# Edge positions of the attention-score one-hots: one line in one partition, spread by a TensorE product

## The reference

```
def _gatv2_layer(x, src, dst, Wl, bl, Wr, br, att, b):
    n = x.shape[0]
    xl = (x @ Wl + bl).reshape(n, H, C)
    xr = (x @ Wr + br).reshape(n, H, C)
    s = jax.nn.leaky_relu(xl[src] + xr[dst], NEG_SLOPE)
    e = jnp.einsum('ehc,hc->eh', s, att)
    ...
```

## Time and profile before

| | us |
|---|---|
| median of 3 runs (3100.20 to 3102.39) | 3101.64 |
| the profiled execution | 3132.41 |
| its span in the trace | 3130.6 |
| the score stage's DVE instructions, layer 0 | from 655.8 |
| the same, layer 1 | from 1775.4 |

### The profile page before, as it was taken

One profiled execution on the slowest core, in us unless ns is written; L12 is line 12 of the kernel. 1 busy time (PEld: TensorE's weight loads), 2 busy tenths in 40 slices (PEclk: granted clock), 3 DMA queues, 4 the chain that ended last, 5 costly groups with the idle time before them and its releaser, 6 DMA issues. The chain is left out here.

```text
span 3130.6 us, 52451 instructions
## 1 busy us (share of the span) xinstructions
PE 2350.9 (75%) x12514; PEld 1551.1 (50%) x12628; DVE 2237.7 (71%) x10715; ACT 1249.0 (40%) x2770; POOL 826.8 (26%) x883
## 2 busy tenths in 40 slices
PE   3775796578888788737885788887788378857999
PEld 1443684234444444416664344444444156645777
DVE  5667666868888888884558688888888944466654
ACT  1776893332222222213354523222222123356654
POOL 0000100036666566500000265666665100000000
PEclk8999898789999999969997899999999689978999
DMA  0000600269999999617543489999988065436221
GB/s 26 1 2 3 282 7 15 91 202 277 276 278 275 271 274 278 193 29 177 159 111 83 159 266 273 277 275 282 275 274 270 4 155 160 137 86 251 80 64 38
DMA packets 418141, 519.14 MB, mean 166 GB/s; under 512 B 31943, under 2 KB 353090, under 8 KB 416450
## 3 DMA queue, kind: packets, MB, share of 16 engines
q0 software_dynamic: 66560, 274.39, 28.0%
q1 hardware_dynamic: 349996, 239.60, 26.4%
q10 hardware_dynamic: 1302, 1.80, 0.2%
HBM read 414.74 MB, written 100.93 MB: 165 GB/s over the span
## 5 line engine op out<-in xcount | busy, mean ns | idle before, releaser
L963 POOL DMA_INDIRECT rows<-row_table,idx x832 | 789.2, 949 | 813.5 <-POOLq L140 307.8
L1014 PE MATMUL z_ps<-xr,hot_ta 128*128 x2400 | 673.6, 388 | 246.1 <-DVE rows L1065 196.6
L1025 PE MATMUL z_ps<-rows,ident 128*128 128x256 f32 x1664 | 576.5, 428 | 10.4 <-issue 10.4
L1014 PEld LDWEIGHTS z_ps<-xr,hot_ta 128*128 128x128 bf16 x2496 | 245.0, 98 | 538.9 <-issue 407.9
L1065 DVE SCALAR_TENSOR_TENSOR rows<-rows,att_all 128x128 f32<-128x128 f32 x1664 | 429.5, 294 | 77.7 <-remote 37.1
L1090 DVE TENSOR_TENSOR rows<-z_ps,rows 128x256 f32<-128x256 f32 x832 | 347.5, 418 | 132.7 <-PE z_ps L1025 89.4
L1065 DVE SCALAR_TENSOR_TENSOR rows<-z_ps,att_all 128x128 f32<-128x128 f32 x1664 | 410.0, 280 | 25.5 <-issue 25.3
L1405 PE MATMUL acc_m<-xr,hot_m 128*128 x1984 | 341.2, 293 | 76.3 <-issue 53.2
L1405 PEld LDWEIGHTS acc_m<-xr,hot_m 128*128 128x128 f32 x1984 | 281.9, 194 | 142.0 <-issue 136.6
L1036 ACT ACTIVATE spread_a<-spread_a,below 128x512 bf16<-128x512 bf16 x208 | 149.9, 721 | 447.8 <-PE z_ps L1025 379.9
L1025 PEld LDWEIGHTS z_ps<-rows,ident 128*128 128x128 f32 x1664 | 257.3, 195 | 112.0 <-issue 18.3
(11 more groups left out here) (460 smaller groups left out, 3673.6 us busy)
## 6 DMA issues: line engine op xcount, KB each, us to landing
xr<-kept_rows SPq DMA_DIRECT2D x124, 512.0 KB
kept_rows<-rows SPq DMA_DIRECT2D x416, 128.0 KB
spread_a<-rel_rows SPq DMA_DIRECT2D x208, 128.0 KB
counts_line<-counts SPq DMA_DIRECT2D x1, 19550.0 KB
counts<-counts_line SPq DMA_DIRECT2D x6, 3200.0 KB, 10.0
rows<-row_table,idx POOLq DMA_INDIRECT x832
row_table<-xl_ring SPq DMA_DIRECT2D x50, 258.0 KB
rows<-row_table SPq DMA_DIRECT2D x32, 320.0 KB, 7.0
```

The lines of the kernel that those rows point to most:

```text
L963: nc.gpsimd.indirect_dma_start(out=rows[:, u, :], out_offset=None, in_=table, in_offset=bass.IndirectOffsetOnAxis(ap=c.idx[:, n:n + 1], ax ...
L1014: nc.tensor.matmul(ps[:, n % Z, :], hot, tile[:, m, 0:HC], start=m == 0, stop=False, skip_group_check=True)
L1025: nc.tensor.matmul(ps[:, n % Z, HALF_C:HC], c.ident[:, :], rows[:, n % ROWS, HALF_C:HC], start=False, stop=True, skip_group_check=True).th ...
```

## The change

SP loads the 512 numbers of a half as one line into one partition (`line`, four buffers, L971). PE multiplies a row of 128 ones (`one_row`, set once by DVE) with that line: a matmul with one row of weights and 512 columns, whose result, in the new PSUM bank `spread_ps`, holds the line in each of the 128 partitions. ACT's Abs reads that bank and writes the same `spread` buffer as before; Relu is unchanged. PE makes the products of halves 0 and 1 ahead of slot 0, and that of half k+2 in slot 4k+1, behind L1019 and ahead of the wait for the gather. It waits there for the Abs of the half before (`apart`), since there is one bank, and for the load (`line`). ACT waits for the product (`spread`, now one counter). SP's wait before a load is for the product that read the buffer. For the bank, `Z` goes from 6 to 5, so PE waits for slot n-5 instead of n-6.

```
--- before.py
+++ after.py
@@ -928,25 +928,29 @@
 
 
 
-    Z = 6
+    Z = 5
     ROWS = 14
     HOTS = 3
+    LINES = 4
     LOAD = HALF
     GROUPS = SLOTS // GROUP
     HALVES = SLOTS // HALF
     with ExitStack() as ctx:
         hot_t = ctx.enter_context(nc.sbuf_tensor(fresh(nc, "hot_ta"), [P, HOTS, HALF * P], BF16))
         spread = ctx.enter_context(nc.sbuf_tensor(fresh(nc, "spread_a"), [P, HOTS, HALF * P], BF16))
+        line = ctx.enter_context(nc.sbuf_tensor(fresh(nc, "rel_line"), [1, LINES, HALF * P], BF16))
+        one_row = ctx.enter_context(nc.sbuf_tensor(fresh(nc, "one_row"), [1, P], BF16))
         below = ctx.enter_context(nc.sbuf_tensor(fresh(nc, "below"), [P, 1], F32))
         part = ctx.enter_context(nc.sbuf_tensor(fresh(nc, "edge_part"), [P, 2, GROUP, H], F32))
         side = ctx.enter_context(nc.sbuf_tensor(fresh(nc, "side"), [P, 2, GROUP, PARTS, H], F32))
         half_sum = ctx.enter_context(nc.sbuf_tensor(fresh(nc, "half_sum"), [P, GROUP, H], F32))
         lin = ctx.enter_context(nc.sbuf_tensor(fresh(nc, "lin"), [P, 2, GROUP, H], F32))
         ps = ctx.enter_context(nc.psum_tensor(fresh(nc, "z_ps"), [P, Z, BANK], F32))
+        spread_ps = ctx.enter_context(nc.psum_tensor(fresh(nc, "spread_ps"), [P, BANK], F32))
         side_ps = ctx.enter_context(nc.psum_tensor(fresh(nc, "side_ps"), [P, 2, BANK], F32))
         rows = ctx.enter_context(nc.sbuf_tensor(fresh(nc, "rows"), [P, ROWS, ROW], F32))
 
-        with phase(nc, used=0, gathered=ROWS, spread=HOTS, below=0, apart=0, hot_t=0, z=0, sides=0, side=0, lin=0, added=0, summed=0,
+        with phase(nc, used=0, gathered=ROWS, line=LINES, one_row=0, spread=0, below=0, apart=0, hot_t=0, z=0, sides=0, side=0, lin=0, added=0, summed=0,
                    vec=0, kept=ROWS // 2) as (block, s):
 
 
@@ -968,18 +972,18 @@
             @block.sync
             def _(sp):
                 def load(k):
-                    sp.dma_start(spread[:, k % HOTS, :], bass.AP(rel_rows.tensor, k * HALF * P,
-                                                                 [[0, P], [1, HALF * P]]))\
-                      .then_inc(s["spread"][k % HOTS], 16)
-
-                for k in range(HOTS):
+                    sp.dma_start(line[:, k % LINES, :], bass.AP(rel_rows.tensor, k * HALF * P,
+                                                                [[HALF * P, 1], [1, HALF * P]]))\
+                      .then_inc(s["line"][k % LINES], 16)
+
+                for k in range(LINES):
                     load(k)
                 for n in range(0, SLOTS, 2):
                     k = n // HALF
-                    if n % HALF == 0 and k + HOTS < HALVES:
-
-                        sp.wait_ge(s["hot_t"], k + 1)
-                        load(k + HOTS)
+                    if n % HALF == 0 and k + LINES < HALVES:
+
+                        sp.wait_ge(s["spread"], k + 1)
+                        load(k + LINES)
                     at = n % ROWS
                     for u in range(at, at + 2):
                         sp.wait_ge(s["gathered"][u], 16 * (n // ROWS + 1))
@@ -996,6 +1000,17 @@
                         max_val=NODE_TILES - 1,
                         skip_runtime_bounds_check_because="slots hold node tiles by construction")[1]
 
+                def spread_rows_of(k):
+
+                    if k > 0:
+                        pe.wait_ge(s["apart"], k)
+                    pe.wait_ge(s["line"][k % LINES], 16 * (k // LINES + 1))
+                    nc.tensor.matmul(spread_ps[:, :], one_row[:, :], line[:, k % LINES, :], start=True, stop=True)\
+                      .then_inc(s["spread"], 1)
+
+                pe.wait_ge(s["one_row"], 1)
+                for k in range(HOTS - 1):
+                    spread_rows_of(k)
                 tiles_next = tiles_at(0)
                 for n in range(SLOTS):
                     u, k = n % GROUP, n // HALF
@@ -1021,6 +1036,8 @@
                         .rearrange("p (n k) -> p n k", n=PARTS), hot, tile[:, :, HC:XRW], start=True, stop=True)
                     if u == GROUP - 1:
                         last.then_inc(s["sides"], 1)
+                    if n % HALF == 1 and k + HOTS - 1 < HALVES:
+                        spread_rows_of(k + HOTS - 1)
                     pe.wait_ge(s["gathered"][n % ROWS], 16 * (n // ROWS + 1))
                     nc.tensor.matmul(ps[:, n % Z, HALF_C:HC], c.ident[:, :], rows[:, n % ROWS, HALF_C:HC],
                                      start=False, stop=True, skip_group_check=True).then_inc(s["z"], 1)
@@ -1029,11 +1046,11 @@
             def _(act):
                 def one_hot(k):
 
-                    act.wait_ge(s["spread"][k % HOTS], 16 * (k // HOTS + 1))
+                    act.wait_ge(s["spread"], k + 1)
                     if k >= HOTS:
                         act.wait_ge(s["z"], (k - HOTS + 1) * HALF)
                     mine = spread[:, k % HOTS, :]
-                    nc.scalar.activation(mine, mine, ACT.Abs, bias=below[:, 0:1]).then_inc(s["apart"], 1)
+                    nc.scalar.activation(mine, spread_ps[:, :], ACT.Abs, bias=below[:, 0:1]).then_inc(s["apart"], 1)
                     act.wait_ge(s["apart"], k + 1)
                     nc.scalar.activation(hot_t[:, k % HOTS, :], mine, ACT.Relu, bias=1.0, scale=-1.0)\
                       .then_inc(s["hot_t"], 1)
@@ -1082,6 +1099,7 @@
                             out=c.e[:, k * GROUP:(k + 1) * GROUP, 0:H], in0=part[:, k % 2, :, :], scalar=1.0 - SLOPE,
                             in1=lin[:, k % 2, :, :], op0=ALU.mult, op1=ALU.add).then_inc(s["summed"], 1)
 
+                nc.vector.memset(one_row[:, :], 1.0).then_inc(s["one_row"], 1)
                 nc.vector.tensor_scalar(below[:, :], c.part[:, 0:1], -1.0, None, ALU.mult).then_inc(s["below"], 1)
                 for n in range(SLOTS):
                     u, k = n % GROUP, n // GROUP
```

8 lines of the change are left out of this document (6 added, 2 removed).

## The result

The changed kernel took 3125.1 us (median of 5 runs, 3122.98 to 3128.0), the kernel before on the same chip 3102.4 (5 runs, 3100.2 to 3109.9): ratio 1.007, 95% interval 1.0057 to 1.0083. The change costs 22.7 us, 0.7%. Forecast were 3028; the range ended at 3125.

The account below looks back on a forecast made before the run. The prediction took the score stage as paced by its DMA transfers, through pauses. Broadcast load -75 us and layer starts +2, the product at nothing, gave -73 us from the median 3101.6: 3028 us, range 2965 to 3125, forecast's own 2995 to 3055.

Parts of the forecast that it names:

- I read the stage as paced by its transfers: Score stage of both layers: 0.28 us of each 1.5625 us slot is lost in pauses that come with DMA traffic.
- -75 us: Score stage: dropping the broadcast load saves 0.103 us per slot, times 0.91, over 804 slots; bounds 50 and 102 us.
- Full DMA traffic and progress of the engines exclude each other: Start and end of the score stage: engines stall at 357 GB/s; with little traffic the lost 0.28 us is gone.
- taken as 0.37 us and 76 us: PE's added product every fourth slot: 56 to 100 us of PE time, 0.09 per slot, counted as costing nothing.
- the thinnest cover of the sum: PE's idle time in the score stage, 110 of 600 us, said to hide the added product.
- Rival A: Slower: PE bounds the score stage, so the product's 76 us add in full, plus 2: 3180 us; chance 0.24.
- its low form, 3130: Rival A with the low DMA price of 50 us given back: 3130 us.
- Rival B: No change: score-stage traffic isn't at its limit, byte cost and product are hidden; 3102 to 3108 us; chance 0.08 with D.
- C: Score-stage pauses shrink more than the bytes: 2877 us at DVE's bound, 2990 for half, PE's floor 2950; chance 0.18.
- D: The one-partition load may be cut into as many packets as before; the gain falls away; chance 0.08 with Rival B.
- Five banks, Abs from PSUM, the line load and the waits at nothing: Score stage: these side effects cost zero; five banks at worst 0.05 us per slot, 40 us.
- Start of each layer, +2: First product at the low clock, its hand-over and the memset add 0.5 to 1.5 us per layer, twice: +2 us.

Follow-up runs that it names:

- P: Kind of chip ("for its pauses") on which the kernel before takes medians of 3102 to 3125 us.
- e18: Kernel before with every tenth slot's gather left out after the first 14 slots: 3004.8 us against 3102.6, ratio 0.9683, on P.
- e10: Kernel before without the broadcast loads of edge positions in the loop, nothing put in their place: 3127.9 us against 3124.7, ratio 1.0018, on P.
- Q: Kind of chip ("quick") on which the kernel before takes medians of 2860 to 2863 us.
- e11: The changed kernel again, no edit, against the kernel before: 3144.4 us against 3124.7, ratio 1.006, on P.
- e4: Changed kernel without the products of halves 2 to 103 of each layer and the waits for them: 2860.2 us, ratio 0.9994, on Q.
- e8: Kernel before with five z banks and one extra product per half that nobody reads or waits for: 3144.0 us, ratio 1.0057, on P.

## Why the prediction was wrong

- **"I read the stage as paced by its transfers"**: half right. On P the pace goes with one kind of them, the gathers; e18 moves more bytes per second than before and is quicker.
- **"-75 us" for the broadcast load: the step that failed.** Three choices stand in it. The price per byte was taken from q0's time and given to q1's packets; the share of 0.91 was taken as the bound; and the pace was made proportional to it. Measured: +3 us, interval -1 to +12 (e10). The queue's time per byte isn't fixed: q0 went from 51.3 to 54.3 ns per 1,000 bytes when the others left (e10).
- **"Full DMA traffic and progress of the engines exclude each other"**, from the start and the end of the stage: both places also differ in their gathers. At the end none is issued any more. Read so, says gathers as well as it says bytes, and I chose bytes.
- **The product "taken as 0.37 us and 76 us", "I cost it at nothing"**: the size was near (0.41, so 85 us), the cover was not whole. On Q its cover is PE's lead over the pace of the slots, 5.00 - 4.76 = 0.24 us per half, so 0.17 come through, 33 us. On P a quarter comes through (20 to 23 of 85 us) and the rest falls into PE's idle time; why a quarter isn't shown. The sentence that PE's idle time is "the thinnest cover of the sum" held. Two readings behind these terms were off, without changing the sign: the 0.27 us of a 512-column matmul has the drain of the last one in it (0.217 without), and PE's 1.275 us per slot lacks the 45 matmuls that the trace doesn't have, an estimated 0.03 us.
- **Rival A** has the mechanism and the sign. Its price of +76 in full was too high on both chips, and its low form, 3130, was built from 50 us of gain that doesn't exist; it lay 5 us from the result by two errors that nearly cancelled. Its deciding point was PE's idle time per slot shrinking by less than 0.09 us. It shrank by 0.059 (e10 against e11), so it did decide the sign; but the larger part of the product was absorbed, which "a fixed part of PE's slot" excluded. The earlier trace rows and the rows of after, with their offset of 27 us and the missing matmuls in one of them, would have said 0.10 and so the opposite.
- **Rival B** is right on the bytes and wrong on the product, which it called hidden.
- **C** was wrong, **D** too.
- **Five banks, Abs from PSUM, the line load and the waits at nothing**: the first three right together on Q (e4). On P they and the waits come to nothing in sum, as e8 with five banks and the product costs what the whole does; singly they weren't tried there. **Start of each layer, +2**: after the change the first z matmul of layer 0 starts at 657.23, 2.9 us behind POOL's first gather of the stage at 654.34; before at 660.41, 3.8 us behind its first gather at 656.57; layer 1 shows the same 2.9 and 3.8. That is a gain of 0.9 us per layer in spite of two products of 0.58 and 0.60 us at the low clock (0.50 of the full one granted from 655 to 661 us), too small to tell in the whole.

Left open: why the gathers go at 1.556 us on some chips and 1.25 on others. The Trainium skill (HBM Reference, Specifications (TRN2)) says that two cores share a memory domain, about 358 GB/s for each when both stream; no run here shows whether another core was at work on P, and P's 275 to 282 GB/s lie well below that share. Open too: which engine's record hides the wait: POOL's idle time names DVE, DVE's names PE, PE's names DVE, as in the earlier trace rows, and none of the three is the cause. Also untried is the kernel without its kept rows, which move as many packets as all else: a later stage reads them.

## What to carry to other kernels

When engines blame each other in a ring and the DMA is nearly full, take away one kind of transfer at a time before putting a price on bytes: here, on P, 33 KB per slot less were worth 0 us as a broadcast and 98 us as gathers, and on Q the same bytes were worth 0 taken away and cost 72 added. An engine's idle time covers an addition only as far as its lead over the next bound goes; on Q 0.24 us per four slots is less than one 0.41 us matmul. A broadcast of one line through TensorE isn't free on an engine that does a slot in 1.19 us where the next one needs 1.25.

## What the runs showed of the hardware

- The same kernel took 3102 to 3125 us on some chips and 2860 on others, within 0.4% on each. With half of the gathers left out 22 us of the 265 remain. The sign of the change was the same on both kinds, its size 20 and 33 us.
- On P there are places where several engines stop together and are released together. Timeline of the kernel after, one such place:

```profile
836.19 0.38 PE L1008 MATMUL spread_ps<-rel_line,one_row 1*128 1x512 bf16 x1
...
836.50 0.70 PE L1042 MATMUL z_ps<-rows,ident 128*128 128x256 f32 x2
838.17 0.29 DVE L1082 SCALAR_TENSOR_TENSOR rows<-rows,att_all 128x128 f32<-128x128 f32 x1 [2.69 <-remote]
838.29 0.25 SPq L975 DMA_DIRECT2D rel_line<-rel_rows  x1
838.29 0.69 ACT L1053 ACTIVATE spread_a<-spread_ps,below 128x512 bf16<-128x512 f32 x1 [6.21 <-PE z_ps L1042]
```

  In the program SP and ACT wait here for the product, which by its record is over at 836.57 (for ACT the view guesses L1042, over at 837.20). Both go on at 838.29, and DVE, which waited for a result of its own, at 838.17. The transfers go on meanwhile, at 340 GB/s from 836.9 to 838.1. POOL has about 100 stops of over 0.6 us in 360 gathers of the kernel before, 1.4 us each in the mean; only half of them fall together with such a stop of DVE, so they aren't all of this kind. On Q, where DVE is busy 398.6 of 400 us, POOL has none.
- A 1 x 512 product between other matmuls costs 0.41 to 0.43 us of PE's time, with waits before it or without, and 512 columns within a run of equal ones 0.217.
- Time per gathered byte fell on Q to 44.8 ns per 1,000 (73.7% of 6,400 engine-us for 105.39 MB in the kernel before), against 51.2 on P, with more traffic at the same time.
